# A decoder layer on one core: residual rows added by an identity product and evicted with their sum by ScalarE, and products that signal their bank directly

## The reference

```
x = layernorm(x + mamba(x))          # W_in, conv of 4 taps, silu, W_x, softplus(dt W_dt),
                                     # state = exp(dt A) state + dt B h   (16 states, 1024 channels, 512 steps)
                                     # y = (C state + D h) silu(gate), then W_out
x = layernorm(x + x softmax(q k^T)^T)   # q, k from the context, 512 rows and columns
x = layernorm(x + ffn(x))            # x and weight rounded to int8 levels, times both scales, + bias
```

## Time and profile before

| | us |
|---|---|
| median of 3 timed runs | 1163.89 (1163.69 to 1163.90) |
| profiled execution, time | 1165.72 |
| its span | 1163.90 |
| its granted TensorE clock, mean | 0.874 |
| TensorE busy | 830.5 (71%) |
| VectorE busy | 1026.1 (88%) |
| ScalarE busy | 759.5 (65%) |
| GpSimd busy | 748.2 (64%) |

### The profile page before, as it was taken

How to read it: one execution, slowest core, us unless ns; L and a number is a source line. 1 busy time by engine, 2 the same in 40 slices (tenths; PEclk the granted TensorE clock), 3 DMA queues, 4 the chain that set the end, 5 groups by cost and what they waited for, 6 DMA issues and landing times.

```text
span 1163.9 us, 10065 instructions
## 1 busy us (share of the span) xinstructions
PE 830.5 (71%) x2708; PEld 327.9 (28%) x2718; DVE 1026.1 (88%) x781; ACT 759.5 (65%) x1164; POOL 748.2 (64%) x419
## 2 busy tenths in 40 slices
PE   7923387877349689987459698987459657567884
PEld 2311032332024234432114233432114223222331
DVE  2569999999989998999989998899998999999833
ACT  3345567776536777786737686787655776777546
POOL 1027666667757856687766866677767867787433
PEclk9976789998679899999769899999859878787997
DMA  5174344453983343453992444344793353234000
GB/s 179 38 182 116 78 110 114 116 140 84 226 225 82 96 104 91 104 136 82 233 257 64 100 102 106 92 122 108 197 248 73 77 141 81 70 88 134 9 0 37
DMA packets 66681, 135.01 MB, mean 116 GB/s; under 512 B 13120, under 2 KB 19392, under 8 KB 66624
## 3 DMA queue, kind: packets, MB, share of 16 engines
q1 hardware_dynamic: 65904, 134.28, 45.6%
q10 hardware_dynamic: 720, 0.08, 0.0%
HBM read 62.75 MB, written 4.46 MB: 58 GB/s over the span
## 4 chain that ended last, share of the span: by engine, by line
issue 35%; DVE 28%; PE 22%; DMA 6%; ACT 5%; POOL 2%; SPq 2%; DVEq 0%; POOLq 0%; ACTq 0%
DVE st L767 19%; PE dense L866 15%; DVE dBu L761 4%; PE dense L922 3%; DMA wide<-w_out 2%; DMA Bb<-bc_rows 2%; PE dense L899 2%; DVE x L726 1%; DVE hs L745 1%; POOL st L456 1%; PE dBu L876 1%; SPq L340 1%; DVE xsc L818 1%; DVE dense L850 1%; ACT squares L592 1%
## 5 line engine op out<-in xcount | busy, mean ns | idle before, releaser
L456 POOL TENSOR_TENSOR st<-st,Cb 128x1024 f32<-128x1024 f32 x250 | 584.5, 2360 | 279.3 <-DVE dBu L761 256.0
L767 DVE TENSOR_TENSOR_SCAN st<-dA,dBu 128x1024 f32<-128x1024 f32 x256 | 570.0, 2266 | 0.0
L568 ACT ACTIVATE dA<-rep,Aneg 128x511 f32<-128x511 f32 x512 | 329.3, 710 | 119.9 <-DVE st L767 110.7
L761 DVE TENSOR_TENSOR dBu<-rep,Bb 128x1024 f32<-128x1024 f32 x250 | 344.9, 1423 | 37.9 <-DMA rep<-steps 10.9
L866 PE MATMUL dense<-xTs,Win 128*128 128x512 f32 x512 | 239.1, 611 | 14.7 <-DMA xTs<-xT 7.8
L899 PE MATMUL dense<-st,sel 128*32 128x512 f32 x1024 | 134.2, 665 | 112.8 <-POOL st L456 112.8
L866 PE MATMUL dense<-wide,hs 128*128 128x512 f32 x256 | 123.4, 640 | 37.9 <-DMA wide<-w_out 37.1
L866 PEld LDWEIGHTS dense<-xTs,Win 128*128 128x128 f32 x512 | 98.3, 196 | 147.2 <-issue 146.5
L922 PE MATMUL dense<-pj,Win 128*128 128x512 f32 (+1 forms) x192 | 94.5, 638 | 32.4 <-issue 22.2
L480 POOL TENSOR_TENSOR steps<-steps,hs 128x512 f32<-128x512 f32 x32 | 57.6, 1799 | 72.8 <-ACT steps L556 72.7
L568 ACT ACT_TABLE_LOAD x62 | 79.5, 1283 | 28.6 <-DVE st L767 24.2
(11 more groups left out here) (104 smaller groups left out, 754.6 us busy)
## 6 DMA issues: line engine op xcount, KB each, us to landing
rep<-steps SPq DMA_DIRECT2D x512, 128.0 KB, 2.4
Win<-w_in SPq DMA_DIRECT2D x64, 256.0 KB, 2.8
wide<-w_out SPq DMA_DIRECT2D x4, 2048.0 KB, 9.9
Win<-w_conv SPq DMA_DIRECT2D x24, 256.0 KB, 2.9
wide<-bc_rows SPq DMA_DIRECT2D x24, 256.0 KB, 6.5
xTs<-xT SPq DMA_DIRECT2D x4, 1024.0 KB, 7.6
Bb<-bc_rows SPq DMA_DIRECT2D x16, 256.0 KB, 7.3
Cb<-bc_rows SPq DMA_DIRECT2D x16, 256.0 KB, 5.8
```

What stands on the lines that cost most here:

```text
L456: nc.gpsimd.tensor_tensor(s, s, C[:, j, :], ALU.mult).then_inc(s_p, 1)
L568: nc.scalar.activation(dA[:, u % 2, j, 1:T], rep[:, u % REPS, 0, 1:T], ACT.Exp, scale=Aneg[:, u % UNITS, j:j + 1]).then_inc(s_dA, 1)
L761: V.tensor_tensor(dBu[:, j, :], rep[:, u % REPS, 1:2, :].to_broadcast([P, JH, T]), B[:, j, :], ALU.mult).then_inc(s_mul, 1)
L767: V.tensor_tensor_scan(st[:, u % RING, j, :].rearrange("p j t -> p (j t)"), dA[:, u % 2, j, :].rearrange("p j t -> p (j t)"), dBu[:, j, :] ...
```

## The change

For wo, av and wp TensorE starts each product with one more pair, the identity times the rows themselves, so that the bank holds product and residual. VectorE adds nothing there any more. ScalarE evicts the bank into the rows with `accum_out` as row sum (`summed`) and does `moments` at once, in the same step; wp is a plain copy. In the last batch wo adds the rows with wp in them again as its residual. `normalize` of wo and av stays one step later; for ff moments stay one step behind, and rstd, normalize and the store each go one step later. Mean times rstd moves from GpSimd to ScalarE, ahead of `normalize`. Waits for the loaded x move from VectorE to TensorE. Finishes, ff adds, gates, convolutions and score exponentials raise `s_free` themselves; who waited for their own semaphores waits for `s_free` (`product_read`, `hidden_ready`). The memset of `ones` and the semaphores that have no more use go.

The diff without the declarations of semaphores and the memset:

```diff
@@ -285,6 +282,13 @@
             eng.wait_ge(s_free[slot], n + 1)
+
+        def hidden_ready(eng, b, e):
+
+            if b:
+                product_read(eng, ("c", b, e))
+            else:
+                eng.wait_ge(s_hs, e + 1)
 
...
@@ -380,8 +384,8 @@
                 ff_at = (REST_AFTER if b == NB else REST)["ff"]
-                if b >= 1 and g - NORM_LAG - 1 in ff_at:
-                    i = ff_at.index(g - NORM_LAG - 1)
+                if b >= 1 and g - NORM_LAG - 2 in ff_at:
+                    i = ff_at.index(g - NORM_LAG - 2)
                     sp.wait_ge(s_ln3, TT * (b - 1) + i + 1)
...
@@ -455,28 +458,25 @@
 
-            rows = []
-            for b, g in STEPS:
+            rows = {}
+            for s, (b, g) in enumerate(STEPS):
                 u = UNITS * b + g + 1
...
                     weigh_states(u, 0)
-                for key in rows:
+                for key in rows.pop(s, []):
 
...
                     nc.gpsimd.tensor_tensor(rstd[:, c], var[:, c], neghalf[:], ALU.pow).then_inc(s_rstd, 1)
-                    pool.wait_ge(s_rstd, 2 * n + 1)
-                    nc.gpsimd.tensor_tensor(nmean[:, c], nmean[:, c], rstd[:, c], ALU.mult).then_inc(s_rstd, 1)
-                rows = []
                 for key in items(b, g):
...
                         pool.wait_ge(s_dt, n + 1)
-                        pool.wait_ge(s_hs, n + 1)
+                        hidden_ready(pool, kb, i)
                         nc.gpsimd.tensor_tensor(steps[:, n % 3, 1, :], steps[:, n % 3, 0, :], hs[:, kb % 2, i, :],
...
@@ -486,11 +486,11 @@
                     if key in norm:
-                        rows.append(key)
+                        rows.setdefault(s + NORM_LAG + (kind == "ff"), []).append(key)
                 if scanned:
...
 
-        NMASKS = 4 + 1 + 7
+        NMASKS = 3 + 1 + 7
 
...
@@ -542,9 +542,7 @@
                 ps, free = full(("c", b, i))
-                nc.scalar.activation(hs[:, b % 2, i, :], ps, ACT.Silu, bias=cb[:, i:i + 1]).then_inc(s_hs, 1)
-                act.wait_ge(s_hs, NE * b + i + 1)
-                act.sem_inc(free, 1)
+                nc.scalar.activation(hs[:, b % 2, i, :], ps, ACT.Silu, bias=cb[:, i:i + 1]).then_inc(free, 1)
 
...
@@ -584,7 +582,8 @@
                 c = slice(n % 4, n % 4 + 1)
-                act.wait_ge(s_sum, n + 1)
+                if key[0] == "ff":
+                    product_read(act, key)
                 nc.scalar.activation(nmean[:, c], rowsum[:, c], ACT.Identity, scale=-1 / H).then_inc(s_mean, 1)
...
@@ -595,10 +594,24 @@
 
+            def summed(key):
+
+                n = norm[key]
+                if n >= 4:
+                    normalized(act, norm_keys[n - 4])
+                ps, free = full(key)
+                nc.scalar.activation(rows_of[key[1]][:, key[2], :], ps, ACT.Identity,
+                                     accum_out=rowsum[:, n % 4:n % 4 + 1]).then_inc(s_raw, 1)
+                act.wait_ge(s_raw, sum(k[0] != "ff" for k in norm_keys[:n + 1]))
+                act.sem_inc(free, 1)
+
             def normalize(key):
...
                 x_i = rows_of[key[1]][:, key[2], :]
-                act.wait_ge(s_rstd, 2 * n + 2)
+                c = slice(n % 4, n % 4 + 1)
+                act.wait_ge(s_rstd, n + 1)
+                nc.scalar.activation(nmean[:, c], nmean[:, c], ACT.Identity, scale=rstd[:, c]).then_inc(s_cent, 1)
+                act.wait_ge(s_cent, n + 1)
                 nc.scalar.activation(x_i, x_i, ACT.Identity, scale=rstd[:, n % 4:n % 4 + 1],
...
@@ -641,8 +654,14 @@
                     key = (kind, kb, i)
-                    if key in norm:
+                    if kind == "wp":
+                        copied(key, rows_of[kb][:, i, :], lambda ps: ps)
+                    elif kind == "ff":
                         norms.setdefault(s + NORM_LAG, []).append(("moments", key))
+                        ends.setdefault(s + NORM_LAG + 1, []).append(key)
+                    elif kind in ("wo", "av"):
+                        summed(key)
+                        moments(key)
                         ends.setdefault(s + NORM_LAG, []).append(key)
...
@@ -660,9 +679,7 @@
                         ps, free = full(key)
-                        nc.scalar.activation(temp_slot(key), ps, ACT.Silu).then_inc(s_gate, 1)
-                        act.wait_ge(s_gate, NE * kb + i + 1)
-                        act.sem_inc(free, 1)
+                        nc.scalar.activation(temp_slot(key), ps, ACT.Silu).then_inc(free, 1)
                     elif kind == "w":
...
@@ -687,9 +704,7 @@
                         nc.scalar.activation(att_of[kb][:, i % 2, :], ps, ACT.Exp, bias=nmax[:, i % 2:i % 2 + 1],
-                                             accum_out=esum[:, i % 2:i % 2 + 1]).then_inc(s_ex, 1)
-                        act.wait_ge(s_ex, TT * kb + i + 1)
-                        act.sem_inc(free, 1)
+                                             accum_out=esum[:, i % 2:i % 2 + 1]).then_inc(free, 1)
                     elif kind == "at":
...
@@ -718,14 +733,13 @@
 
-            def add_rows(key, x_i, ps):
+            def add_rows(key, x_i, ps, free):
 
...
                 V.scalar_tensor_tensor(x_i, ps, 1.0, x_i, ALU.mult, ALU.add,
-                                       accum_out=rowsum[:, n % 4:n % 4 + 1]).then_inc(s_sum, 1)
-                dve.wait_ge(s_sum, n + 1)
+                                       accum_out=rowsum[:, n % 4:n % 4 + 1]).then_inc(free, 1)
 
...
@@ -741,11 +755,9 @@
                 ps, free = full(("y", b, e))
-                dve.wait_ge(s_gate, NE * b + e + 1)
+                product_read(dve, ("g", b, e))
                 V.tensor_tensor(hs[:, b % 2, e, :], ps, ta[:, temp[("g", b, e)] % TEMPS, :],
-                                ALU.mult).then_inc(s_y, 1)
-                dve.wait_ge(s_y, NE * b + e + 1)
-                dve.sem_inc(free, 1)
+                                ALU.mult).then_inc(free, 1)
 
...
@@ -805,9 +817,9 @@
                     key = (kind, kb, i)
-                    x_i = rows_of[kb][:, i, :] if kind in ("wp", "wo", "av", "ff") else None
+                    x_i = rows_of[kb][:, i, :] if kind == "av" else None
                     if kind == "en":
-                        dve.wait_ge(s_ex, TT * kb + i + 1)
+                        product_read(dve, key)
                         if i >= 2:
...
@@ -822,26 +834,17 @@
                     key = (kind, kb, i)
-                    x_i = rows_of[kb][:, i, :] if kind in ("wp", "wo", "av", "ff") else None
+                    x_i = rows_of[kb][:, i, :] if kind == "ff" else None
                     if kind == "h" and kb == 0:
...
                         if i >= 2:
-                            dve.wait_ge(s_ex, TT * kb + i - 1)
+                            product_read(dve, ("en", kb, i - 2))
                         V.tensor_reduce(nmax[:, i % 2:i % 2 + 1], ps, AX_X, ALU.max, negate=True).then_inc(s_mx, 1)
                         norms.setdefault(s + 1, []).append(key)
-                    elif kind in ("wp", "wo", "av"):
-                        if kind in ("wp", "wo") and i == 0:
-                            dve.wait_ge(s_xr, 16 * (kb + 1))
-                        ps, free = full(key)
-                        if kind == "wp":
-                            link(V.tensor_tensor(x_i, ps, x_i, ALU.add))
-                        else:
-                            add_rows(key, x_i, ps)
-                        dve.sem_inc(free, 1)
-                        if kind == "av":
-                            norms.setdefault(s + QUANT_LAG, []).append(key)
+                    elif kind == "av":
+                        norms.setdefault(s + QUANT_LAG, []).append(key)
                     elif kind == "ff":
...
@@ -849,8 +852,7 @@
                         dve.wait_ge(s_xb, TT * kb + i + 1)
-                        add_rows(key, x_i, ps)
-                        dve.sem_inc(free, 1)
+                        add_rows(key, x_i, ps, free)
 
...
@@ -929,7 +931,8 @@
                         pe.wait_ge(s_wx, 16 * (kb + 1))
-                        pe.wait_ge(s_hs, NE * (kb + 1))
+                        for e in range(NE):
+                            hidden_ready(pe, kb, e)
                         product(key, [(Wx[:, e, 0:TR], hs[:, kb % 2, e, :]) for e in range(NE)])
...
@@ -964,8 +967,13 @@
                             pe.wait_ge(s_wout, 16 * (kb + 1))
-                            pe.wait_ge(s_y, NE * kb + end)
-                        product(key, [(hs[:, kb % 2, e, cols], Wout[:, e, :]) for e in range(first, end)])
+                            pe.wait_ge(s_xr, 16 * (kb + 1))
+                            for e in range(first, end):
+                                product_read(pe, ("y", kb, e))
+                        if first:
+                            product_read(pe, ("wp", kb, i))
+                        product(key, [(ident[:], rows_of[kb][:, i, :])]
```

(4 more changed lines are left out.)

12 lines of the change are left out of this document (4 added, 8 removed).

## The result

The changed kernel takes 1181.61 us (median of 4 runs, 1178.74 to 1182.69) against 1163.89: 1.0143 times as long, 95% interval 1.0119 to 1.0167. The forecast was 1156.2, faster, with a range that ended at 1168. It was wrong in sign and in range. The profiled execution took 1178.74, with a span of 1176.8. It is the fastest of the four: the spans of the two traces differ by 12.9 us, the medians by 17.7.

A forecast was written before the change was run, and what follows sets the result against it. VectorE was taken as the scan's bound, TensorE and ScalarE as setting the pace after it. Batch 0 2.2, batches 1 and 2 10.0, batch 3 9.3, tail -13.8: 7.7 us less, 1156.2, range 1144 to 1168.

The forecast's parts named there:

- batch 0: First batch, which has only finishes: 7 x 0.32 = 2.2 us gained.
- the signals: VectorE in the scan: without self-wait 31 finishes gain 0.32 us each and 12 ff adds 0.2 each.
- The tail (-13.8): Stage after the scan: 13.8 us lost, 4.9 on the way to av0 and 8.8 in two rings.
- the two rings: After the scan, av0 to av1 and av1 to av2: 8.3 us each instead of 3.9, 8.8 lost.
- wo, 5.5 a batch and two finishes: Steps 2 to 8 of a batch: VectorE 5.5 us ahead at unit 10, 6.1 with two finishes.
- Carried on by the same prices: Within wo's steps: wo1 to wo3 give about 2.3 us more, less 0.5 for the GpSimd overrun.
- With the last finishes a batch ends 5.0 us ahead, twice: End of batches 1 and 2: about 5.0 us gained in each, 10.0 together.
- The stores of ff rows come one step later and wait on nothing that VectorE needs: ff rows stored one step later in the scan: no cost counted.
- av in batches 1 and 2: Steps 15 to 25: TensorE is the next bound, and VectorE's lead falls to 4.5 us.
- gain nothing: The wp adds, in the last four units of batch 3: removing them gains nothing.
- the slower one: Rival: ScalarE's order bounds batches 1 and 2, VectorE waits for TensorE's c, h and y; 1169.5 us, chance 0.16.
- The rival that the tail does not ring: After the scan evictions overlap the next products, so 6 us are lost instead of 13.8; 1148 us, chance 0.11.

The follow-up runs named there:

- e1: Kernel before plus only the change's direct signals; wo, av, wp added by VectorE, mean times rstd on GpSimd, ff at its old step: 1150.25 us.
- f1: Kernel before plus direct signals, identity for wo of batches 0 to 2, and z with its softplus ahead of wo at steps 2 and 6: 1141.52 us.
- f2: Kernel before plus direct signals, all rows added by VectorE, and z ahead of wo at steps 2 and 6: 1146.17 us.
- e10: Kernel before plus direct signals, with only rstd, normalize and store of ff rows one step later, as in the change: 1154.09 us.
- e5: The changed kernel, but with rstd, normalize and store of ff rows back at the old step: 1171.34 us.

## Why the prediction was wrong, step by step

- **What bounds the kernel; batch 0; the signals:** right. Batch 0 gave 2.7 where 2.2 was forecast, a finish 0.32 where 0.32 was, an ff add 0.32 where 0.2 was. The prediction never summed this part alone, and e1 doesn't measure it alone either: its 13.65 has the adds' own signals in it.
- **The tail (-13.8):** right in mechanism; that the size came out at 14.1 in the profile (63.95 - 49.89; 16.8 in the medians) is in part luck. The way to av0 gave 4.5 (4.9 forecast), the two rings 10.5 (8.8), and from av3's product to the end it was 1.0 less (nothing forecast). The first ring took 8.32 as worked out (8.3); what was left out is that the second ran with TensorE's clock down and took 10.01.
- **wo, 5.5 a batch and two finishes:** mis-sized, 18.3 in the sum and 4.6 in the trace. The walk was right up to unit 5: batch 2's lead goes -0.2, 4.3, 3.2 at units 3, 4, 5, so 3.4 were gained where it said 3.7. The step that failed is "Carried on by the same prices": it looked at ScalarE's softplus only as something ahead of the exponentials and forgot who else waits for it. GpSimd's product with z is ahead of its weighings, so they slide into VectorE's next dBu, for which 0.5 was put in all; the pair of unit 6 took 6.12, 4.50 and 6.58 in batches 1 to 3 instead of 2.7. The waits for late exponentials ahead of it (2.52, 0.45 and 2.05 at unit 5) are the smaller part. With z ahead of wo (f1) both go, and the leads grow by 3.3, 4.5 and 4.8 from unit x.3 to x.10, where without the identity (f2) they grow by 0.5, 2.6 and 2.1. The whole of dBu grew by 14.7, where some 4 were put down.
- **"With the last finishes a batch ends 5.0 us ahead, twice":** the lead at the end of batch 1 was 5.86 where 7.2 was forecast, but it was assumed to pass to the next batch. The earlier trace rows have no row of the boundary; in the kernel before the first dBu already waited 1.33 for B there, that is, the way over dt, B, C and the stage loads was the bound already, and what VectorE leads beyond it is lost. The change lost 10.4 at two places. With the 13.7 of wo this is the missing 20 of the scan, less some 4 us gained elsewhere.
- **"The stores of ff rows come one step later and wait on nothing that VectorE needs":** it has no bearing on the store alone (0 to 0.8 us a boundary), but the step it speaks of, ff's rstd and normalize included, gave 10.3 when undone in the change and 3.8 alone (e10). The way from dt to B and C gets longer by it, and its TensorE clock lower (0.88 in the change and 1.00 in e5, in the stretches above). Why the clock fell there, and how much of the 10.3 it is, stays open; no run moved the normalize without the store.
- **av in batches 1 and 2:** the chain through TensorE was there (the lead falls from 11.4 to 5.9 between units 17 and 18 of batch 1); from 1.10 to 1.31 nothing was gained (5.9 to 5.9; -1.1 was forecast), and from 2.10 to 2.31 1.8 were lost. Batch 3's +5.2 from unit 10 on was more than the 3.2 put down.
- **wp, "gain nothing":** it costs, 3.0 by the medians, 2.2 of it in the last finish's wait for y. The 0.9 to 2.7 worked out for it were hidden behind "GpSimd's last products hide half".
- **The rivals:** the slower one had the right sign and its place, ScalarE's order in the scan. Its mark came in part: scans waited 5.0 in all for exponentials, two of the three times longer than the 1.5 us that the prediction named as a sign of being wrong. But it had the damage go over TensorE's c, h and y; it went through z to GpSimd's weighings and through dt to the loads, and its 1169.5 left both out. The rival that the tail does not ring is refuted by the 8.32 and 10.01.
- **"A measurement tells about 0.2%":** too narrow. Eleven runs of the kernel before lie between 1162.0 and 1166.2, the four of the change between 1178.7 and 1182.7.

## What to carry to other kernels

Price a change that has several parts for each part alone: here the smallest looking one (a signal given by the instruction itself, on the remaining adds too) was worth 13.7 us, and the change as a whole is 31 us slower than that part. A lead that the busiest engine gains is only kept if what starts the next stage's transfers moves with it; look for a first use of loaded data that waits even a little in the kernel before. When work is moved to an engine, look not only at what stands behind it on that engine, but also at the third engine that waits for it.
